# Reordering the last units of a vision tower kernel: coefficient steps, drive blocks, scan steps and the order in which weights are spread

## What is computed

```python
# tokens: one query for each patch of 4x4 pixels, attending over its 16 pixels
x = features.reshape(b, c, h, s, w, s)
reduce_feats = x.mean((3, 5)).reshape(b, c, hw).transpose(0, 2, 1)
q = _ln(reduce_feats, ln_q_w, ln_q_b) @ Wq.T
kv = _ln(unf, ln_kv_w, ln_kv_b) @ Wkv.T
attn = softmax(einsum('bhpd,bhpnd->bhpn', q * scale, k), axis=-1)
aggre = einsum('bhpn,bhpnd->bhpd', attn, v)
h = reduce_feats + aggre @ proj_w.T + proj_b
# recurrence over the 256 tokens of an image
x_new = s * x - dsa * z + fx
z_new = ds * x + s * z + fz
u = h; g = gelu(z @ W_C.T + b_C + u @ W_D.T + b_D)
h = layernorm(h + (g * sigmoid(g) + u))
# experts: shared MLP plus the best two of four
h = layernorm(h + shared + gated)
```

## Time and profile before

| | |
|---|---|
| median of 3 runs | 905.13 us |
| the profiled execution | 904.89 us |
| its span (first to last instruction) | 903.1 us |
| mean granted clock of PE, share of full speed | 0.990 |
| PE busy | 848.0 us (94%) |
| DVE busy | 724.0 us (80%) |
| POOL busy | 524.6 us (58%) |
| ACT busy | 494.8 us (55%) |

### The profile page before, as it was taken

The page is one execution under the profiler, slowest core; times in us unless marked ns, Lnnn a source line. Parts: engine busy times, 40 slices in busy tenths (PEclk is TensorE's granted clock), DMA queues, the critical chain, the costliest instruction groups (busy, mean ns, idle before and its releaser), DMA issues.

```text
span 903.1 us, 23483 instructions
## 1 busy us (share of the span) xinstructions
PE 848.0 (94%) x9144; PEld 354.7 (39%) x9144; DVE 724.0 (80%) x1187; ACT 494.8 (55%) x783; POOL 524.6 (58%) x387
## 2 busy tenths in 40 slices
PE   5799999999999999999999998796999999999996
PEld 2133334334334334334334333354444444444442
DVE  5788788888788788888888888994767878778775
ACT  3555455455455455455455456356756666666662
POOL 2699899999999999999999993200212112111110
PEclk9999999999999999999999999997999999999999
DMA  9578988988988888988978956100000000000000
GB/s 375 156 200 222 260 267 227 253 270 231 253 266 231 257 260 234 256 258 240 261 247 244 259 158 158 28 1 2 1 12 13 20 17 13 24 12 13 24 13 35
DMA packets 49056, 141.60 MB, mean 157 GB/s; under 512 B 5440, under 2 KB 5440, under 8 KB 40768
## 3 DMA queue, kind: packets, MB, share of 16 engines
q1 hardware_dynamic: 48960, 140.21, 52.1%
HBM read 68.88 MB, written 4.19 MB: 81 GB/s over the span
## 4 chain that ended last, share of the span: by engine, by line
PE 37%; POOL 24%; issue 15%; DMA 9%; DVE 7%; SPq 7%; ACT 1%; POOLq 1%; DVEq 0%
DMA sb_arena<-x 7%; SPq L539 6%; POOL sb_prodv L596 5%; PE ring L1176 5%; POOL sb_rows L502 5%; PE ring L1146 4%; PE ring L917 3%; POOL sb_wgt L589 3%; PE bank_ms L1188 3%; POOL sb_score L578 3%; POOL sb_wgt L584 3%; POOL sb_rows L504 3%; PE bank_ms L889 2%; PE qp L1131 2%; PE bank_sq L1176 2%
## 5 line engine op out<-in xcount | busy, mean ns | idle before, releaser
L917 PE MATMUL ring<-sb_arena,sb_wqkv 64*64 64x512 f32 x2048 | 255.6, 603 | 4.9 <-DVE sb_prodv L1348 3.7
L1317 DVE TENSOR_TENSOR sb_prodk<-ring,sb_qbuf 128x1024 f32<-128x1024 f32 x128 | 153.3, 1220 | 18.6 <-PE ring L917 15.4
L644 POOL TENSOR_TENSOR sb_parts_q<-sb_arena,sb_const 128x512 fp32r<-128x512 f32 x15 | 15.6, 1041 | 250.6 <-DVE sb_arena L1554 250.6
L497 POOL TENSOR_TENSOR sb_rows<-sb_arena 128x2048 f32<-128x2048 f32 x31 | 141.7, 4571 | 27.2 <-DVE sb_sum L489 15.8
L1348 DVE TENSOR_TENSOR sb_prodv<-ring,sb_wbc 128x1024 f32<-128x1024 f32 x128 | 151.0, 1202 | 1.9 <-issue 1.9
L688 ACT ACTIVATE sb_xsq<-sb_arena 128x2048 f32<-128x2048 f32 x64 | 118.4, 1896 | 1.9 <-DMA sb_arena<-x 1.9
L956 PEld LDWEIGHTS qp<-sb_prodv,sb_tok_w 64*64 64x64 f32 x3072 | 88.9, 133 | 71.1 <-POOL sb_prodv L596 33.9
L917 PEld LDWEIGHTS ring<-sb_arena,sb_wqkv 64*64 64x64 f32 x2048 | 66.1, 133 | 119.2 <-issue 94.5
L956 PE MATMUL qp<-sb_prodv,sb_tok_w 64*64 64x128 f32 x3072 | 101.9, 271 | 10.6 <-POOL sb_prodv L596 8.3
L596 POOL TENSOR_TENSOR sb_prodv<-sb_prodv 128x256 f32<-128x256 f32 x128 | 93.2, 739 | 11.0 <-DVE sb_prodv L1348 11.0
L659 ACT ACTIVATE sb_means<-sb_sum 128x256 f32<-128x256 f32 x32 | 13.3, 417 | 119.2 <-POOL sb_sum L507 115.3
(11 more groups left out here) (246 smaller groups left out, 1443.0 us busy)
## 6 DMA issues: line engine op xcount, KB each, us to landing
sb_arena<-x SPq DMA_DIRECT2D x64, 1024.0 KB, 8.7
sb_wbc<-sb_wgt SPq DMA_DIRECT2D x256, 256.0 KB, 5.3
out<-sb_arena SPq DMA_DIRECT2D x16, 256.0 KB, 2.0
sb_rest_w<-rest_w SPq DMA_DIRECT2D x1, 950.5 KB, 21.5
sb_const<-const SPq DMA_DIRECT2D x1, 264.5 KB, 3.1
sb_tok_w<-tok_w SPq DMA_DIRECT2D x1, 260.5 KB, 2.9
sb_const<-const SPq DMA_DIRECT2D x1, 256.0 KB, 21.7
```

Of the source, the lines that this page charges most:

```text
L497: eng.tensor_tensor(rows[:, :, :, :], pix[:, :, 0:8], pix[:, :, 8:16], ALU.add).then_inc(sum8_ready, 1)
L917: mm = pe.matmul(ring[slot][C * half:C * half + C, i, :], image_block(w, i), x[C * i:C * i + C, m, half, c], start=True, stop=True)
L1317: dve.tensor_tensor(by_pixel(prodk[:, c]), by_pixel(ring[c % 2][:, :, :]), q[:, :, None, :].to_broadcast([P, 2, N_PIX, G32]), ALU.mult).th ...
```

## The change

Four edits:

1. `spread_weights` sends both transfers of a chunk one after the other (c0 c0, c2 c2, then c1 c1, c3 c3), where it alternated between two chunks (c0 c2 c0 c2, then c1 c3 c1 c3). This is for all units.
2. In PE's `last_step` the second value block of unit 31 and `drive(0, 2)` stand ahead of the projections of unit 30, and `drive(0, 3)` behind these projections instead of behind the last value block.
3. `EARLY` is 7 instead of 5 and `BEFORE_TOKENS` 10 instead of 9: six scan pairs ahead of the tokens of unit 30 in place of four, three (7 to 9) between the last value products and the last tokens in place of four (5 to 8), six behind in place of seven.
4. The three levels of `far_steps` go from the last step to steps 28, 29 and 30, one each, behind the tokens and ahead of `score_scale`.

```diff
@@ -534,8 +534,8 @@
                 sp.wait_ge(weights_ready, u + 1)
                 for k in range(0, NC, 2):
                     sp.wait_ge(values_weighted, count(NC * (u - 1) + k + 2))
-                    for i in range(2):
-                        for c in VALUE_ORDER[k:k + 2]:
+                    for c in VALUE_ORDER[k:k + 2]:
+                        for i in range(2):
                             sp.dma_start(wbc[:, c, i, :],
                                          wgt[32 * c + i:32 * c + 32:2, None, :].to_broadcast([16, D, CH])
                                          ).then_inc(weights_spread[c], 16)
@@ -1022,13 +1022,13 @@
             def last_step(n, m):
                 drive(0, 1)
                 values(n, m, 0)
+                values(n, m, 1)
+                drive(0, 2)
                 for part in range(N_SUM // N_PART):
                     project(n - 1, part)
-                values(n, m, 1)
-                drive(0, 2)
+                drive(0, 3)
                 values(n, m, 2)
                 values(n, m, 3)
-                drive(0, 3)
                 for part in range(N_SUM // N_PART):
                     project(n, part)
 
@@ -1424,7 +1424,7 @@
                     dve.scalar_tensor_tensor(chunks(dst[o], d + 1, NCK), chunks(src[1], own, NCK - 1 - d + own), coef[o][:, 1:2],
                                              chunks(jump_tmp[o], d + 1, NCK), ALU.mult, ALU.add).then_inc(carry_step[h], 1)
 
-            EARLY, BEFORE_TOKENS = 5, 9
+            EARLY, BEFORE_TOKENS = 7, 10
 
             query_var(0)
             query_scaled(0)
@@ -1453,6 +1453,8 @@
                         scan_on(0, j)
                 if not isinstance(n, int) or n >= 1:
                     tokens(n - 1, (m - 1) % NF)
+                if isinstance(n, int) and UNITS - NF <= n < UNITS - 1:
+                    far_steps(n - (UNITS - NF))
                 if nxt:
                     score_scale(n + 1)
                     score_max(n + 1)
@@ -1464,9 +1466,6 @@
                     query_var(n + 2)
                 if nxt:
                     score_inverse(n + 1)
-                if not nxt:
-                    for level in range(3):
-                        far_steps(level)
                 value_products(n, m, 2)
                 if nxt2:
                     query_scaled(n + 2)
```

## The result

The changed kernel took **915.69 us** in the median (five runs, 913.72 to 919.56); the kernel before, beside it on the same chip, 905.86 us (five runs, 905.05 to 908.37). The ratio is 1.011, with a 95% interval of 1.0086 to 1.0134: slower by some 1%, where 902.1 was forecast. The profiled execution took 918.41 us, 2.7 more than the median; its span is 916.6 us against 903.1. So the trace shows a difference of 13.5 us, and the medians one of 9.8.

The account below looks back on a forecast made before the run. PE bounds units until 550 us, DVE the end from 557.6. Holes and coefficient steps of 4.43 us, less 1.1 of new waits and 0.4 of stretching, gave 2.9; against 3.15 counted by steps, 3.0 was taken: 902.1 us, range 901.2 to 903.2.

Parts of the forecast that it names:

- Order of the transfers: Units other than the last: weights land by 535.3, POOL needs them at 537.18, so the new order costs 0.
- Rival D: Two transfers in a row reading one 32-partition band collide; weights land 4.2 us later each unit, about 936 us; chance 0.04.
- 9.6 us for the eight: Within the band rival: 2.1 MB of weights at some 218 GB/s for one half of the ports, shrinking the gain to about 1.5.
- first product: Last unit's first value product on DVE, behind six scan pairs and unit 30's tokens: starts at 564.05, formerly 564.17.
- waits before the third and fourth product: New DVE waits in the last unit for the weights of chunks 1 and 3: 0.85 and 0.25 us, 1.1 together.
- last tokens: Tokens on DVE after the last unit's value products and three scan pairs: start at 573.0 in place of 575.66.
- carry: PE's last wait for the carry from DVE: at 607.1 instead of 610.08.
- slack of PE: PE's idle time before the terms from the carry: shrinks from 1.66 to 1.3 us, so DVE stays the bound.
- Rival A: Last unit's transfers land by chunk, so the 1.1 us of new waits goes: 4.2 us won, 900.9; chance 0.08.
- The lock of the coefficient steps: Moved coefficient steps in the score holes may wait for POOL, scores 0.4 us late; costed at 0, other end 0.9.
- Rival C: Locks with POOL add up: 0.9 us in score holes, 0.8 more at POOL's setup; 1.3 won, 903.8; chance 0.13.
- Rival B: PE's clock falls ahead of the last projections: 5.7 us instead of 2.85, tokens wait 2.8; 904.9; chance 0.10.

Follow-up runs that it names:

- e5: Kernel before, weights' transfers reading rows in the new order but writing destinations in the old (contents exchanged between chunks): 919.72 us, ratio 1.016.
- e6: Kernel before, weights' transfers writing destinations in the new order but reading rows in the old (contents exchanged between chunks): 907.01 us, ratio 0.9996.
- e7: Kernel before with chunk order 0, 1, 2, 3 for products and transfers, so one half is read four times in a row: 961.88 us, ratio 1.0628.
- e9: Kernel before with value products in order 0, 1, 2, 3 but transfers sent 0 2 1 3 twice, halves in turn: 908.28 us, ratio 1.0024.
- e3: Changed kernel with the new transfer order in the last unit (31) alone, old order in all others: 903.45 us, ratio 0.9971 against the kernel before.
- e2: Changed kernel without its edit to the transfer order (coefficient steps, drive blocks and scan steps only): 904.05 us, ratio 0.9973 against the kernel before.
- e8: Changed kernel with transfers by chunk in the last unit only, all four chunks in turn (0 2 1 3, twice) elsewhere: 902.22 us, ratio 0.9948 against the kernel before.
- e12: Kernel before with only the drive blocks and scan pairs moved (EARLY 7, BEFORE_TOKENS 10): 904.61 us in one run, beside 905.1.
- e10: e8 with one more scan pair ahead of the tokens of unit 30 (EARLY 8, BEFORE_TOKENS 11): 901.61 us, ratio 0.9952 against the kernel before.
- e1: Kernel before with the new order of the weights' transfers in all units and nothing else: 920.9 us, ratio 1.0162.
- e11: Kernel before with only the coefficient steps moved into the score waits: 904.43 us in one run, beside 905.1.
- e4: Kernel before, old transfer order, with two 128-byte transfers ahead of each unit's pixel loads so these are issued later: 907.31 us, ratio 1.0014.

## Why the prediction was wrong

**The step that failed** is the last of the change part by part: "*Order of the transfers* in all other units: … Nothing moves, 0." It asked only when POOL needs the weights (537.18) and found 1.9 us of slack behind the last landing. There it was right: the weights land no later. It did not ask who else is in the same queue. Behind the eight transfers stand the two pixel loads of a later unit, and for them the kernel before had no slack: POOL waited for pixels 22 times, 11.1 us. The prediction does not speak of that row, and the unit that it read, with issues from 523.6, has no pixel load behind it, since the last one is issued at 514.6. The row of before:

```profile
L528 SPq DMA_DIRECT2D sb_arena<-x x64: 422/830/1724, 1.7 to 514.6; - x64
```

So a delay of 0.8 us in the mean, and 1.5 in the unit shown, goes through in most of the 13 long ones of the 31 distances (2 were long before), and in three of these the wait lets PE's clock fall besides: 16.77 us in all, where 0 was put down.

**Its assumption** failed with it, since it was made for too few transfers: "that the n-th transfer issued lands when the n-th did, since the same eight go through the same queue". For the eight themselves it held: in the mean of units 4 to 26 no landing moved by more than 0.55 us, the last one came 0.2 us earlier, and in the last unit the waits were 1.23 us in all, in three pieces, against 1.1 in two. It did not hold for the ninth and tenth transfer in the queue, the pixel loads, which land 0.7 and 0.8 us later. How the reading side brings that about without delaying the eight is not shown; what is shown is the sequence that does it.

**Rival D** had the cause, though in part: "If the reading side of a band is what limits them" is right about the reading side (e5 against e6), and so is the sign that it gives. Three things in it were off. The unit is the half of the partitions, not the band of 32: e7 never reads a band twice in a row and is 6.3% slower. The place where it acts is the pixel loads and through them POOL's additions, not POOL's product of the weights at 537.18. And its price, weights that land 4.2 us later in each unit, was too high: they land no later, and in e7, with four in a row, by 0.6 us. For the loop as a whole it came to 16.8 us instead of 30, by another way. Against it was set that "three or four of them were under way at any time, as they will be now". That is no argument: with three or four under way it matters whether they read both halves. A chance of 0.04 was too low for a question on which no row of before spoke. That the outcome was slower, as this rival had it, is in part luck, since its own path, the weights' landing, did not move.

The Trainium skill (SBUF — State Buffer, Door 1: The DMA port swizzle) gives each half of the partitions its own ports. e7 and e9 agree that the half is what counts: the same bytes, one half four times in a row or both in turn, 961.88 against 908.28 us. The same page of the Trainium skill (section "Can I just issue two DMAs to hit both halves?") says that transfers to the two halves serialize and gain only 6%, and its page DMA: Bandwidth & Descriptors (Rules for kernel authors) says of two such transfers not to bother. Taken over to this stream of transfers, that would make e7 nearly the same as e9. The runs differ by 53.6 us, and the last L1331 by 53.1, about 1.7 us per unit, and the measurement decides. The prediction's 9.6 us for the eight, with its gain of about 1.5, came from the figure of that first section; no run shows it, since the eight took 12.1 us with the halves in turn and 12.7 in e7.

**What held.** The steps on the end of the program, by e3, where the transfers of the other units keep the old sequence: a first product at 564.34 (forecast 564.05, in a kernel whose last unit starts 0.4 later), waits before the third and fourth product of 0.72 and 0.24 (0.85 and 0.25), and one of 0.32 before the second that was not forecast; last tokens at 573.51 (573.0); carry at 607.28 (607.1); slack of PE 1.00 (1.3). The total is 2.9 us (3.0). By the changed kernel's own marks the end gains 3.24. Rival A, by which the waits for chunk 1 and chunk 3 would have gone, did not come.

**The lock of the coefficient steps** came as costed, and a little beyond. Changed kernel, DVE and POOL, the first of the three groups:

```profile
531.85 0.58 DVE L1397 TENSOR_SCALAR sb_cacc<-sb_cv,sb_cz 128x2 f32<-128x2 f32 x1
532.48 1.27 POOL L504 TENSOR_TENSOR sb_rows<-sb_rows 128x512 f32<-128x512 f32 x1
532.59 1.17 DVE L1400 SCALAR_TENSOR_TENSOR sb_far<-sb_cz,sb_cacc 128x2 f32<-128x2 f32 x1
```

The step of 1.17 us starts 0.11 us behind POOL's instruction and ends with it, at 533.76 and 533.75. In e2, where the units keep their length, scores start 0.43 and 0.47 us later behind the start of the last key product than before (3.70 and 3.74 us against 3.27), in two of three units, but the three periods of score maximum to score maximum add up to 50.33 us, three times 16.78. They are absorbed: 0, as costed. Rival C's 0.9 us did not come.

**Rival B** was given 0.10 and happened often. Of the six profiles with the new order at the end, e2, e8 and e12 had a mean clock of 0.61 to 0.64 in the last projections, the changed kernel, e3 and e10 full speed. It does not belong to that order: with the old one the clock was 0.50 to 0.64 there in e1, e6, e7 and e9, 0.86 in e11, and full only in e4, e5 and the kernel before. The waits of PE ahead of the projections hardly tell: 2.06, 0.67 and 1.51 us in e2, 2.08, 0.45 and 2.32 in e3. The forecast price was 2.8 us. The tokens waited 1.4 to 1.6 us in e2, e8 and e12, since the clock comes back before the projections end; in e6, at 0.50 throughout, these took 5.40 us, 2.55 more than at full speed. Each kernel was profiled once: whether this goes with the kernel or with the execution stays open.

## What to carry to other kernels

Before putting the cost of a reordered transfer at nothing, read who is behind it in the queue, and whether that one already waits: the row that decided here was a wait of 11.1 us in 22 pieces for a different tile. Read it in a unit of the middle, where the whole queue is full, and not in one of the last. A wait on the engine that bounds the unit can cost more than itself, when the clock falls behind it: 2.0 us of wait came to 3.3 us here. When small tiles are spread from a few partitions, write down which half of the partitions (0 to 63 or 64 to 127) each transfer in flight reads, and let them take turns. Where an order helps only at the end of the program, use it only there: e3, e8 and e10 keep the gain, and e8 and e10 end 0.5% below the kernel before.

## What the runs showed of the hardware

- Transfers between tiles, reading 16 partitions each: eight of 256 KB that read halves in turn leave the loop as it was (e8, e9); two and two cost 1.6% of the kernel (e1, e5), four and four 6.3% (e7), the falls of the clock behind the waits included. On the writing side, each transfer writing all partitions, the order made no difference (e6, 0.9996).
- An issue on SP is not a fixed cost: issues of the same transfer took 550 to 1343 ns within a unit. Two small transfers ahead of the pixel loads made the loads' issue short (420 ns, e4, against 785 and 945) without moving their landing by as much as they were later.
- A DVE instruction of two elements per partition, 0.21 us in the earlier trace rows, took 1.17 us beside a POOL instruction of 1.27 us and ended with it, where the earlier trace rows had shown 0.565 at most.
- PE's clock fell to half in the loop of the changed kernel behind waits of 1.98, 2.01 and 2.50 us, and stood at full speed behind waits of 0.74 to 1.82 us; in e3 it stood at full speed behind 2.08 and 2.32 us too. In the last projections it fell, in part or throughout, in eight of 14 kernels. In the kernel before it was 0.50 over 565.5 to 568.0 and again over 623.5 to 633.0.
